# Two routed expert layers: fixed regions for the sorted rows, routing in groups of tiles, and results scattered from the expert loop

## What is computed

```python
logits = norm(tokens) @ gate            # 8 experts
rw, re = top_k(softmax(logits), 2)      # layer 0; layer 1: softmax over the two best logits
for e in range(8):
    h = gelu(tokens @ w1[e] + b1[e])    # 256 -> 256 in layer 0, 256 -> 1024 in layer 1
    y = h @ w2[e] + b2[e]               # back to 256
    out = out + combine[:, e:e+1] * y   # combine is zero but for a token's two experts
```

## Time and profile before

| | |
|---|---|
| three runs | 2734.43, 2737.84, 2738.3 us, median 2737.84 |
| the profiled execution | 2757.99 us, of which the span of instructions 2756.3 |
| busy share of the span | PE 75%, DVE 75%, ACT 55%, POOL 33% |
| mean granted TensorE clock | 0.859 of 2.4 GHz |
| moved by DMA | 147.07 MB |

### The profile page before, as it was taken

The page is one execution under the profiler, slowest core; times in us unless marked ns, Lnnn a source line. Parts: engine busy times, 40 slices in busy tenths (PEclk is TensorE's granted clock), DMA queues, the critical chain, the costliest instruction groups (busy, mean ns, idle before and its releaser), DMA issues. The chain is left out here.

```text
span 2756.3 us, 80547 instructions
## 1 busy us (share of the span) xinstructions
PE 2073.8 (75%) x26686; PEld 1558.4 (57%) x26687; DVE 2053.9 (75%) x3051; ACT 1503.3 (55%) x1982; POOL 908.0 (33%) x1023
## 2 busy tenths in 40 slices
PE   4639999999999999999770593036983079999961
PEld 3327666666666666666550472013862069999951
DVE  4979999999999999999782365487985334454433
ACT  5339999999999999999421120022532233333311
POOL 2652111121111111111036445460124844455455
PEclk8869999999999999999855797557975589999975
DMA  1001111111111111111204353200003611111123
GB/s 73 0 23 31 30 30 30 30 29 27 29 29 29 30 30 30 30 30 33 66 1 162 118 159 113 75 1 1 0 0 133 232 60 46 47 52 46 46 77 126
DMA packets 235071, 147.07 MB, mean 53 GB/s; under 512 B 151873, under 2 KB 214417, under 8 KB 234769
## 3 DMA queue, kind: packets, MB, share of 16 engines
q1 hardware_dynamic: 201520, 92.48, 12.9%
q0 software_dynamic: 12288, 33.57, 3.7%
q10 hardware_dynamic: 21216, 20.45, 2.1%
HBM read 70.52 MB, written 51.64 MB: 44 GB/s over the span
## 5 line engine op out<-in xcount | busy, mean ns | idle before, releaser
L579 DVE TENSOR_TENSOR plow<-prob 128x1024 f16<-128x1024 f32 (+1 forms) x1024 | 1128.0, 1174 | 4.9 <-ACT prob L493 4.9
L493 ACT ACTIVATE prob<-scores 128x1024 f32<-128x1024 f32 x1024 | 999.1, 1026 | 91.0 <-PE scores L622 63.3
L642 PEld LDWEIGHTS outp<-vs,prob 128*128 128x128 bf16 x7680 | 516.2, 98 | 277.7 <-issue 215.7
L642 PE MATMUL outp<-vs,prob 128*128 (+1 forms) x7680 | 604.4, 193 | 26.8 <-DVE plow L579 15.9
L622 PE MATMUL scores<-qT,kT 128*128 (+1 forms) x2048 | 611.6, 380 | 7.6 <-DMA kT<-shift_rows 2.8
L644 PE MATMUL outp<-vs,plow 128*128 (+1 forms) x7680 | 601.8, 193 | 0.0
L644 PEld LDWEIGHTS outp<-vs,plow 128*128 128x128 f16 x7680 | 503.4, 97 | 59.4 <-issue 0.5
L441 POOL TENSOR_TENSOR osum<-osb 128x128 f32<-128x128 f32 x64 | 105.2, 1643 | 957.3 <-DVE rec L584 957.3
L1338 ACT ACTIVATE m1ehf<-m1eph,m1eb1c 128x256 f32<-128x256 f32 x312 | 144.8, 475 | 269.5 <-PE m1eph L1294 269.2
L1400 POOL TENSOR_TENSOR m1ehl<-m1ehf,m1ehh 128x256 f16<-128x256 f32 x312 | 211.6, 709 | 219.3 <-DVE m1ehh L1369 219.3
L1294 PE MATMUL m1eph<-m1exT,m1w 128*128 128x256 f16 x1872 | 212.3, 274 | 0.2 <-DVE m1exT L1363 0.2
(11 more groups left out here) (343 smaller groups left out, 3290.3 us busy)
## 6 DMA issues: line engine op xcount, KB each, us to landing
m1estg<-in_L_ffn_W_dram SPq DMA_DIRECT2D x16, 1024.0 KB
sorted_rows<-zero SPq DMA_DIRECT2D x64, 156.0 KB
m0exr<-sorted_rows SPq DMA_DIRECT2D x39, 256.0 KB, 2.7
expert_rows<-m0eyo ACTq DMA_DIRECT2D x39, 256.0 KB, 2.3
m1exr<-sorted_rows SPq DMA_DIRECT2D x39, 256.0 KB, 3.3
expert_rows<-m1eyo ACTq DMA_DIRECT2D x39, 256.0 KB, 3.8
staged<-qk SPq DMA_DIRECT2D x73, 128.0 KB, 2.5
tok<-in_x_dram SPq DMA_DIRECT2D x4, 1024.0 KB, 10.2
```

The lines of the kernel that those rows point to most:

```text
L493: act.activation(prob[g % PBUF][:, :], scores[g % 2][:, :], ACT.Exp, scale=1.0 / (QK_SCALE * QK_SCALE)).then_inc(prob_ready, 1)
L579: dve.tensor_tensor(l[:, 0:n], p[:, 0:n], high(p)[:, 0:n], ALU.subtract).then_inc(low_ready, 1)
L642: pe.matmul(to, high(prob[g % PBUF])[:, cols], v, start=(g == 0 and i == 0 and j == 0), stop=False, skip_group_check=True)
```

## The change

- **The sorted list gets fixed regions.** Each expert has 4096 rows of its own (`REGION`), so that a slot can be given before all tokens are counted. A row is 261 float32 wide: the two halves, the number of the token's first expert, and where its result belongs. Each layer has its own list (34 MB), and the zeroing in the first attention covers both.
- **Routing and sending in groups.** `dispatch` takes the place of `token_norm`, `logits_and_rows`, `route` and the first block of `experts`. ScalarE normalizes, VectorE makes both halves and, in layer 0, adds the row to `tok`; the gate is multiplied in halves too. After every 8 tiles `route(g)` runs on 64 numbers a row and GpSimd sends the group's 16 scatters, out of a ring of 16 tiles. The counts for the table of tiles come last (`tables`).
- **All expert weights are split behind the last group's routing** (`parts_before` is zero for every group but the last, all parts after it), in pieces of at most 1024 columns: 16 of 512 in layer 0, 32 of 1024 in layer 1.
- **The expert loop has 71 tiles of 128 rows.** Its results are scattered by GpSimd straight to row 2 x token + choice. VectorE makes both halves of gelu's result, ScalarE copies the turned rows. b2 is loaded at the block's start.
- **Combine** reads eight plain pieces of 1 MB instead of 64 gathers.

```diff
@@ attention, SyncE @@
-                sp.dma_start(sorted_dram[ds(c * ZP * ZROWS, ZP * ZROWS), :].rearrange("(p a) c -> p a c", a=ZROWS),
-                             zero[0:ZP, :, :]).then_inc(zeroed, 16)
+                for rows in sorted_rows:
+                    sp.dma_start(rows[ds(c * P * ZROWS, P * ZROWS), :].rearrange("(a p) c -> p a c", p=P),
+                                 zero[:, :, :].broadcast_to([P, ZROWS, RW])).then_inc(zeroed, 16)
@@ sizes @@
-ET = 256
+ET = P
+REGION = S
 MAXT = (TOP * S + E_N * (ET - 1)) // ET
+SROWS = E_N * REGION + P
+NR = 4
+RW = D + 1 + NR
+G = 8
+NGR = NT // G
+RING = 2 * G
@@ dispatch: VectorE, ScalarE @@
+            def prepare(t):
+                row = halves[:, t % RING, :]
+                dve.wait_ge(xn_ready, t + 1)
+                if t >= RING:
+                    dve.wait_ge(sent[t % RING], 16 * TOP * (t // RING))
+                dve.tensor_copy(row[:, 0:D], xn[t % NX][:, :]).then_inc(hi_ready, 1)
+                if add_norm:
+                    dve.tensor_tensor(tok[:, t, :], tok[:, t, :], xn[t % NX][:, :], ALU.add)
+                dve.wait_ge(hi_ready, t + 1)
+                dve.tensor_tensor(row[:, D:2 * D], xn[t % NX][:, :], row[:, 0:D], ALU.subtract).then_inc(kept, 1)
...
+        LEAD = 3
+        route_after = {min(g * G + G - 1 + LEAD, NT - 1): g for g in range(NGR)}
+        parts_before = [0] * NGR + [NP]
...
+            for t in range(NT):
+                prepare(t)
...
+                if t in route_after:
+                    g = route_after[t]
+                    route(g)
+                    if g == NGR - 1:
+                        tables()
+                    for i in range(parts_before[g], parts_before[g + 1]):
+                        low(i)
@@ dispatch: GpSimd @@
+            for t in range(NT):
+                pool.wait_ge(slots_ready, t // G + 1)
+                for i in range(TOP):
+                    to = bass.IndirectOffsetOnAxis(ap=slots[t // G % 2][:, i, t % G:t % G + 1], axis=0)
+                    pool.indirect_dma_start(out=sorted_dram, out_offset=to, in_=rows[:, t % RING, :], in_offset=None
+                                            ).then_inc(sent[t % RING], 16)
@@ experts: VectorE, GpSimd @@
+            def aim(i, u, it):
+                e = expert_of(dve, reg, i)
+                dve.wait_ge(x_in[u % NR], (it + u // NR) * 16 + 16)
...
+                    dve.wait_ge(y_out[u % NR], sent_before * 16)
...
+            def step(i, u, it, left):
+                if left > 1:
+                    aim(i + 2, u + 2, it)
+                if left > 0:
+                    halve(i + 1, u + 1)
+                rows_out(i, u)
...
+                pool.wait_ge(aimed, i + 1 + NR)
+                pool.wait_ge(y_taken, i + 3)
+                pool.sem_inc(sending, 1)
+                to = bass.IndirectOffsetOnAxis(ap=dest[u][:, 0:1], axis=0)
+                pool.indirect_dma_start(out=y_dram, out_offset=to, in_=yo[u][:, :], in_offset=None
+                                        ).then_inc(y_out[u], 16)
@@ combine @@
+        src = y_dram[0:TOP * S, :].rearrange("(t p c) d -> p t (c d)", p=P, c=TOP)
+
+        def fetch(eng, q):
+            if q >= NB:
+                eng.wait_ge(added, TOP * GC * (q - NB + 1))
+            eng.dma_start(got[q % NB][:, :, :], src[:, q * GC:(q + 1) * GC, :]).then_inc(arrived[q % NB], 16)
```

More of the change, by code:

```diff
@@ new lines, in dispatch @@
+        r = sb("r", [P, G])
+        best = sb("best", [P, TOP, G])
+        code = sb("code", [P, TOP, G])
+        place = sb("place", [P, TOP, G])
+        slots = [sb(f"slots{u}", [P, TOP, G], I32) for u in range(2)]
+        seen = [sb(f"seen{u}", [P, E_N], F16) for u in range(2)]
+        more = sb("more", [P, E_N])
+        cnt = sb("cnt", [P, E_N])
+        over = sb("over", [P, E_N, S // ET])
+        stops = [sb(f"stops{u}", [P, E_N]) for u in range(2)]
+        tiles = sb("tiles", [P, E_N])
@@ new lines, in _ @@
+            act.wait_ge(eps_set, 1)
+            act.wait_ge(norm_step, 1)
+            act.activation(sd[:, :], mv[:, :, 1], ACT.Sqrt, bias=eps[:, 0:1]).then_inc(rooted, 1)
+            act.wait_ge(norm_step, 3)
+            normed(0)
+            normed(1)
+            for t in range(NT):
+                if t + 2 < NT:
+                    normed(t + 2)
+                take(t)
+                if t + 1 in route_after and t + 1 < NT - 1:
+                    g = route_after[t + 1]
+                    weigh(g)
+                    for i in range(parts_before[g], parts_before[g + 1]):
+                        high(i)
@@ L1128, in _, with turn @@
+            g = route_after[NT - 1]
+            weigh(g)
+            for i in range(parts_before[g], parts_before[g + 1]):
+                high(i)
         @block.tensor
         def _(pe):
-            m = mask[:, :, :].rearrange("p t e -> p (t e)")
-            pe.wait_ge(step, marks["mask"])
-            pe.matmul(pt[:, 0:NT * E_N], ones[:, :], m, start=True, stop=True)
-            pe.matmul(pc[:, 0:NT * E_N], below[:, :], m, start=True, stop=True).then_inc(summed, 1)
-def experts(nc, name, F, w1, shared, rows16, slots, w1_dram, b1_dram, w2_dram, b2_dram, sorted_dram, y_dram,
-            tile_expert, ident16, ident32):
+            def turn(t):
+                pe.wait_ge(kept, t + 1)
+                if t >= 2:
+                    pe.wait_ge(xt_ready, t - 1)
+                for q in range(2 * KB):
+                    last = pe.transpose(px[t % 2][:, q, :], halves[:, t % RING, q * P:(q + 1) * P], ident16[:, :])
+                last.then_inc(turned, 1)
@@ L1321, in step @@
+                last.then_inc(y_ready, 1)
+            def step(i, u, it, left):
+                if left > 1:
+                    turn(i + 2, u + 2, it)
+                if left > 0:
+                    first(i + 1, u + 1)
                 second(i, u)
-            pe.sem_inc(turned, 2)
-            pe.sem_inc(y_ready, 2 * EH)
+            pe.sem_inc(turned, NR)
             turn(0, 0, 0)
@@ L1974, in build @@
         tile_no = sb("tile_no", [P, MAXT], F32)
-        consts = (below, ones, steps, first, tile_no)
+        tok2 = sb("tok2", [P, NT], F32)
+        base = sb("base", [P, E_N], F16)
+        consts = (below, ones, steps, first, tile_no, tok2, base)
         make_identities(nc, ident32, ident16)
```

853 lines of the change are left out of this document (431 added, 422 removed).

## The result

The changed kernel takes 2794.22 us (median of four runs, 2790.08 to 2795.36) against 2736.44 for the kernel before in the same comparison: 1.021 of it, with a 95% interval of 1.019 to 1.023. The forecast was 2580, so sign and size are both wrong. The profiled execution took 2795.36 us, its span is 2793.6.

A forecast was written before the change was run, and what follows sets the result against it. VectorE bound the attention, TensorE the loops; the change works at GpSimd's 256 indirect DMAs. Terms -47 + 46 - 37 - 43 - 33 - 44 = -158 took 2757.99 to 2600 us, 20 less for the median: 2580, range 2540 to 2655.

The forecast's parts named there:

- Loop of layer 1: Layer 1's expert loop: TensorE needs 5.5 us a tile for 71 tiles, 400 us instead of 432.9, 33 less.
- Loop of layer 0: Layer 0's expert loop: the output scatter's flight sets a 2.4 us step, 182 us instead of 135.6, 46 more.
- Head of layer 0: Layer 0's norm, routing, sending and splitting: scatters end at 110 us, weights at 113; 118 instead of 165.2, 47 less.
- Combines: Both layers' combines: layer 0 bound by VectorE, 55 us, 37 less; layer 1 by transfers, 54 us, 44 less.
- Head of layer 1: Layer 1's head: 32 weight pieces behind the routing, one in 2.0 us; 148 us instead of 190.8, 43 less.
- rival 5: Layer 1's head: weights are the bound after all, 2.6 us a piece, 19 us more, total 2599; chance 0.06.
- Attention: First attention: zeros of 1.07 MB a chunk take 4 us within 12 us of empty queue, so no change.
- Rival 4: First attention: zeros outlast their 12 us cover and lengthen 64 chunks; at 16 us 256 more, total 2836; chance 0.04.
- Rival 1: Layer 0's loop: the clock falls to half, a tile takes 3.1 us, 62 us more, total 2642; chance 0.15.
- Rival 2: Layer 0's head and loop: GpSimd emits scatters more slowly beside VectorE, 38 and 21 us more, total 2639; chance 0.15.
- the 0.95 for "faster": Whole kernel: chance 0.95 of being faster by more than 5 us, 0.01 within that, 0.04 slower.
- if a step of layer 1's loop exceeds 5.6 us: Layer 1's loop: one of three signs that would show the prediction wrong; a step was put at 5.5 us.

The follow-up runs named there:

- e1: The changed kernel with TensorE's `first` always taking w1 at a fixed address (expert 0) in both layers; 2649.67 us, 0.963 of the kernel before.
- e2: The kernel before with `first` taking w1 at a fixed address (expert 0); 2756.28 us, 1.000 of the kernel before.
- e4: The changed kernel with 8 instead of 4 buffers for the loop's input rows, output rows and destinations; 2848.53 us, 1.034 of the kernel before.
- e9: The changed kernel with destinations computed one tile ahead instead of two, behind the scatter of three tiles back; 2810.14 us, 1.020 of the kernel before.
- e13: The kernel of e9 with `first` also taking w1 at a fixed address (expert 0); 2623.85 us, 0.953 of the kernel before.
- e6: The changed kernel with a fourth staging buffer for weight pieces, laid over the normalized rows; 2774.39 us, 1.013 of the kernel before.

## Why the prediction was wrong

- **Loop of layer 1 (-33 forecast, +128 measured): the step that decided.** "Matmuls of 128 columns start 0.055 us apart with a new weight each time" was read from a loop whose weights stand at fixed addresses, and carried to one where a register chooses them. e1 makes the sum come true (5.52 a tile for the forecast's 5.50), e2 shows why the kernel before gave no warning: its 256 columns covered the address instructions. The sum counted every instruction of a tile but those, although the order of instructions has them; the step of the prediction that failed is this term, 48 x 0.055 = 2.64 us a tile for what took 4.40. Of the missed 161 us, 155 are this.
- **Loop of layer 0 (+46, +79).** The mechanism, the line and the form of the sum, (flight + step) / 2, were right; the flight was mis-sized, 2.78 for 4.15 us. Pick-up was 0.79 instead of the 0.30 between two scatters that were both ready, landing 2.40 instead of 1.52. With 4.15 the formula gives (4.15 + 2.06) / 2 = 3.1, near the 2.9 measured. Behind it stood a step of 2.6, where the forecast had 1.54 for TensorE and 2.06 for VectorE: e4 and e9, without the wait, get only to 197 and 202. 0.47 us of that step are the same address instructions (e9's mean step is 2.64, e13's 2.17, and `first` takes 1.12 there instead of 12 x 0.055 = 0.66).
- **Head of layer 0 (-47, -43)** held in its parts: the last scatter ends 109 us after the head's start (forecast 110) and the weights at 111 (113), and it is 11 us from there to the first matmul (8). Some of the agreement in the difference is luck, since the profiled execution of the kernel before had long heads. **Combines (-37, -42; -44, -54)**: layer 0's held; layer 1's took 44.5 us, all of it at 283 GB/s, so that the 11 us put on top of the transfers for begin and end weren't there.
- **Head of layer 1 (-43, -32).** A piece took 2.4 us on average (the last 28 in 66 us), between the forecast's 2.0 and rival 5's 2.6, since it needs 4.5 us to land with three under way and not 1.8 + 1.5 = 3.3. VectorE came to the weights at 80 us instead of 74. The forecast's sum names three pieces loaded ahead and doesn't take them off: 74 + 58 + 10 is 142, not 148, so the miss is larger than it looks. e6 shows that buffers are what was short. Part of the -32 is the long head in the profiled execution of the kernel before.
- **Attention** was rightly put at nothing: the first stretch of the table is that of the earlier trace rows to 0.1 us on VectorE, with 128 zeroing transfers of 522 KB under it. Rival 4, the only one given for the slow side, didn't occur; the cost that turned the sign was one that no rival named.
- **Rival 1** is refuted: the clock is 0.97 over layer 0's loop with TensorE busy 159 of 214 us, and 1.00 from 1540 to 1660. **Rival 2**: scatters take 0.96 us on average in both loops (68.20 / 71), 1.02 in layer 0's head, next to nothing. The trap of VectorE blocking GpSimd's DMAs (the Trainium skill, SBUF — State Buffer, the "DVE blocks DMA" trap), if it was at work there, thus cost less than 4 us.
- The range and the 0.95 for "faster" rested on rivals that all varied the size of known terms. What the text named as a sign of failure, "if a step of layer 1's loop exceeds 5.6 us", is what came.

## What to carry to other kernels

When tiles are made smaller, count what comes per tile and not per row, the address and register instructions too, and hold each run of them against the time of the matmuls around it: here one address instruction for three matmuls of 128 columns was all but free and two were not. A longer loop body has a price too: here eight long tiles in one body were fetched anew in every round. A pace read from one loop holds for another only if the instructions between are the same. A wait for an indirect DMA is to be priced from the producer's end to the consumer's start (4.15 us here), and moving it moves the release of whatever the same instruction reads.

## What the runs showed of the hardware

- Address instructions on TensorE: 16 among 48 matmuls of 128 columns cost these 0 to 0.04 us, 24 cost 0.70, 32 cost 1.56; 32 among 48 of 256 columns nothing.
- A loop body of eight tiles in layer 1, some 1600 instructions on TensorE, costs a pause of 7 us at every restart, and nine packets of 16 KB of instructions are fetched in each round; one of half that pauses no more than 0.5 us and is fetched once.
- Weight-loading heads took 8 and 20 us longer in the groups in which the kernel before took 2755 instead of 2740 us, with the same loops.
- Writing 68 MB of padding rows (128 x 522 KB) under VectorE's attention, with 82 GB/s moved in all instead of 30, cost no measurable time.
